# A two-layer decoder: stack loads ahead of value loads, normed rows and slots placed a step or more later, and four heads' scores at a time in the last two groups of each attention stage

## The reference, cut to what matters

```
x = layernorm(x + self_attention_0(x))          # "a0", causal, 16 heads of 16
x = layernorm(x + cross_attention_0(x, ctx))    # "c0", 1024 keys
x = layernorm(x + soft_moe(x))                  # rms-normed rows and slots, 8 experts
x = layernorm(x + self_attention_1(x))          # "a1", causal
x = layernorm(x + cross_attention_1(x, ctx))    # "c1", 1024 keys
y = layernorm(x, g1, b1)
x = x + attention_2(y); x = layernorm(x + token_moe(layernorm(x, g2, b2)))   # "a2", causal
```

## Time and profile before

| | us |
|---|---|
| median of 3 runs (2868.8 to 2877.04) | 2875.1 |
| the profiled execution, its own time | 2872.66 |
| its span | 2870.9 |

### The profile page before, as it was taken

The page is one execution under the profiler, slowest core; times in us unless marked ns, Lnnn a source line. Parts: engine busy times, 40 slices in busy tenths (PEclk is TensorE's granted clock), DMA queues, the critical chain, the costliest instruction groups (busy, mean ns, idle before and its releaser), DMA issues. The chain is left out here.

```text
span 2870.9 us, 47221 instructions
## 1 busy us (share of the span) xinstructions
PE 2526.0 (88%) x15793; PEld 1449.9 (51%) x15794; DVE 1494.8 (52%) x4176; ACT 1330.3 (46%) x2833; POOL 444.9 (15%) x687
## 2 busy tenths in 40 slices
PE   6999999999869889997899999999987994499991
PEld 3555544444334456675456544444444553266661
DVE  2555877888544500023555788777745654222224
ACT  2655466667744412111455567666664551022220
POOL 4222221101100000000123212202122001400004
PEclk8999999999999999999899999999998995599996
DMA  7544534233000022114644533242132317311103
GB/s 222 160 134 137 141 85 103 52 78 78 1 1 0 1 95 93 62 48 141 178 131 127 144 93 93 60 107 85 47 94 83 97 51 249 128 33 33 33 29 94
DMA packets 153825, 259.89 MB, mean 91 GB/s; under 512 B 22713, under 2 KB 96705, under 8 KB 149441
## 3 DMA queue, kind: packets, MB, share of 16 engines
q1 hardware_dynamic: 150544, 248.81, 29.9%
q0 software_dynamic: 3072, 8.39, 0.9%
HBM read 180.71 MB, written 81.53 MB: 91 GB/s over the span
## 5 line engine op out<-in xcount | busy, mean ns | idle before, releaser
L1444 ACT ACTIVATE second_p<-psum 128x512 f32<-128x512 f32 (+3 forms) x1024 | 461.5, 522 | 250.4 <-PE psum L1286 246.9
L1444 ACT ACTIVATE first_p<-psum 128x512 f32<-128x512 f32 (+3 forms) x768 | 366.7, 548 | 180.0 <-PE psum L1286 177.2
L1536 DVE TENSOR_REDUCE second_max_parts<-psum 128x1 f32<-128x512 f32 x512 | 323.0, 684 | 72.5 <-PE psum L1263 70.7
L1536 DVE TENSOR_REDUCE first_max_parts<-psum 128x1 f32<-128x512 f32 x512 | 323.0, 684 | 62.6 <-PE psum L1263 61.2
L1532 DVE CUSTOM_DVE_ANT_0 second_masked<-psum,mask_qk 128x384 f32<-128x384 f32 (+3 forms) x512 | 229.3, 488 | 198.1 <-PE psum L1263 168.0
L1298 PE MATMUL psum<-second_p,second_v_aug 128*32 128x512 f32 (+3 forms) x2048 | 236.0, 533 | 8.7 <-ACT second_p L1444 8.3
L1263 PE MATMUL psum<-second_k,second_q 64*128 64x512 f32 (+3 forms) x1024 | 201.0, 390 | 40.1 <-DMA second_k<-a_k_parts 27.4
L1276 PE MATMUL psum<-second_q,second_k 64*128 64x512 f32 (+3 forms) x1024 | 224.1, 434 | 3.3 <-DVE second_max_parts L1536 1.0
L1286 PE MATMUL psum<-second_shift_T,choose 64*128 64x512 f32 (+3 forms) x1024 | 196.9, 380 | 0.0
L1298 PE MATMUL psum<-first_p,first_v_aug 128*32 128x512 f32 (+3 forms) x1536 | 185.6, 555 | 10.5 <-ACT first_p L1444 10.5
L1276 PEld LDWEIGHTS psum<-second_q,second_k 64*128 64x128 f32 x1024 | 97.4, 186 | 186.0 <-ACT second_p L1444 78.1
(11 more groups left out here) (337 smaller groups left out, 3759.2 us busy)
## 6 DMA issues: line engine op xcount, KB each, us to landing
first_k<-c_k_parts SPq DMA_DIRECT2D x64, 256.0 KB, 4.7
second_q<-a_q_parts SPq DMA_DIRECT2D x128, 128.0 KB, 2.9
second_k<-a_k_parts SPq DMA_DIRECT2D x128, 128.0 KB, 2.9
second_k<-c_k_parts SPq DMA_DIRECT2D x64, 256.0 KB, 4.8
first_q<-a_q_parts SPq DMA_DIRECT2D x64, 128.0 KB, 2.9
first_k<-a_k_parts SPq DMA_DIRECT2D x64, 128.0 KB, 2.9
c_k_parts<-first_held SPq DMA_DIRECT2D x16, 512.0 KB, 3.0
first_q<-c_q_parts SPq DMA_DIRECT2D x64, 128.0 KB, 4.4
```

The lines of the kernel that those rows point to most:

```text
L1444: evacuated(act.activation(probs[tile % 2][:, 2 * h + p, q0:SEQ], bank[:, q0:SEQ], ACT.Exp, scale=scale), event)
L1536: evacuated(v.reduce_max(max_parts[n % 2][:, h, p, qt, k0 // BANK:k0 // BANK + 1], bank[:, 0:width], axis=AX_X), event)
```

## The change

It edits only the list of events. No operation is added or taken away.

```diff
--- before.py
+++ after.py
@@ -790,6 +790,10 @@
         steps = layer.key_tiles
         for t in range(steps):
             plan.append(("scores", n, (t, 0)))
+            if n + 2 >= groups:
+                if t == steps - 1 and n + 1 < groups:
+                    plan.append(("shift", n + 1, 0))
+                plan.append(("scores", n, (t, 1)))
             share(units, 2 * t + 1, 2 * steps)
             if t:
                 plan.append(("values", n, t - 1))
@@ -800,13 +804,14 @@
                     plan.append(("turn", n - 1, 0))
                 if n + 1 < groups:
                     plan.append(("augment", n + 1, 0))
+                if NB <= n + 3 < groups:
+                    plan.append(("load", n + 3, 0))
                 if n + 3 < groups:
                     plan.append(("vload", n + 3, 0))
-                if NB <= n + 3 < groups:
-                    plan.append(("load", n + 3, 0))
-            if t == steps - 1 and n + 1 < groups:
-                plan.append(("shift", n + 1, 0))
-            plan.append(("scores", n, (t, 1)))
+            if n + 2 < groups:
+                if t == steps - 1:
+                    plan.append(("shift", n + 1, 0))
+                plan.append(("scores", n, (t, 1)))
             share(units, 2 * t + 2, 2 * steps)
             if n + 1 < groups and t < 3:
                 plan.extend([("chain", n + 1, 2 * t), ("chain", n + 1, 2 * t + 1)])
@@ -2388,7 +2393,7 @@
             else:
                 pieces[GROUPS * (slot + 1)] = output_pieces(c0, slot) + rms_pieces(slot)
         pieces[GROUPS * BATCH + GROUPS - 1] += [("slot_stats", 0, 0), ("slot_root", 0, 0)]
-        pieces[GROUPS * BATCH + GROUPS] = [REST] + slot_pieces()
+        pieces[GROUPS * BATCH + GROUPS] = [REST, REST] + slot_pieces()
         soft_ctx = ctx.enter_context(ExitStack())
         c.rows = soft_ctx.enter_context(nc.sbuf_tensor("soft_rows_kept", [P, NT, D], F32))
         c.xT = soft_ctx.enter_context(nc.sbuf_tensor("soft_xT_kept", [P, DK, T], F32))
@@ -2430,11 +2435,14 @@
             whole = front_pieces(a2, slot, "x")
             pieces[first + 1] = output_pieces(c1, slot - BATCH)
             if b < BATCH - 1:
-                pieces[first + 2] = [REST, REST] + scaled_rows(slot) + whole[:5]
-                pieces[first + 3] = whole[5:]
+                pieces[first + 2] = [REST] * 3 + scaled_rows(slot) + whole[:4]
+                pieces[first + 3] = whole[4:]
             else:
-                pieces[first + 3] = scaled_rows(slot) + whole[:5]
-                pieces[first + 4] = whole[5:]
+                apply = pieces[first + 1].pop()
+                pieces[first + 2] = [REST, apply, REST, REST]
+                pieces[first + 3] = [REST, REST] + scaled_rows(slot) + whole[:3]
+                pieces[first + 4] = whole[3:7]
+                pieces[first + 5] = whole[7:] + pieces[first + 5]
             first += NG
             pieces[first + (b < BATCH - 1)] = output_pieces(a2, slot)
         fills = [(rows_dram[at:min(at + T, TILES * P), :], x_rows[0:min(T, TILES * P - at), :], rows_filled)
```

## The result

The changed kernel takes 2830.14 us, the median of 4 runs (2821.3 to 2832.26), beside 2874.65 for the kernel before in runs of the same time; the ratio is 0.9842 [0.9816, 0.9868], so 1.6% faster. The forecast of 2828 is 2 us off. The profiled execution took 2821.3 us (span 2819.5) and is the fastest of the four, so the two profiled executions differ by 51.4 us where the medians differ by 44.5. The experiment "after_again" says what the other 7 are. Medians leave out one disturbed execution, of rows_apart, which took 3262.4 us at a granted clock of 0.734.

What follows compares the result with a forecast made beforehand. The prediction took TensorE's work plus its waits to be the bound, with only waits and half clock to gain. Its terms, 5.3 + 6.2 + 4.4 + 12.0 + 2.0 + 0 + 11.0 + 3.5 = 44.4, took 2872.66 to 2828 us, range 2820 to 2837.

Steps and rivals of the forecast that it cites:

- slots 8 to 10: Second stage: TensorE's waits for VectorE's row operations shrink as turns move a step away; 6.2 us gained, ends 2.8 and 8.
- slot 11: Second stage: the 10.11 us stack wait goes, a wait of about 4.4 for rows stays; 12.0 us gained, ends 9 and 14.
- group 37: Output projections stop waiting right behind their turns, with a half step now between them; 2.0 us gained, ends 1 and 2.
- first tail: Groups 30 and 31 of "first": steps of 2.90 us become 2.05 to 2.2; 11.0 us gained, ends 7 and 12.4.
- second tail: Groups 46 and 47 of "second": seven waits of up to 0.89 us shrink; 3.5 us gained, ends 2 and 4.6.
- Part A: Stack transfers issued ahead of values on SyncE: small stack waits gain 5.3 us, ends 3 and 8; the 10.11 goes too.
- the clock behind them: TensorE's half-speed work after the waits at slots 8 to 10: 4.4 of 5.8 us gained, ends 0 and 5.8.
- Rival 2: Moved rows trade waits: evacuation costs 2 us per slot, clock still falls; terms 6.2 and 4.4 become 2.8 and 0; chance 0.15.
- Part C: The slots' first turn, 4.54 us behind VectorE's eight row operations: nothing gained, 0 us, ends -1 and 1.
- Part B: Last two groups of each stage, four heads' scores ahead of the values: 11.0 us in "first", 3.5 in "second".
- Rival 1: ScalarE becomes the bound in the last groups, steps stay near 2.5 us, 5 of 14.5 us gained; 2838, chance 0.12.
- Rivals 3 and 4: Stacks late by bandwidth, 10.11 stays, 2846, chance 0.04; early stack transfers collide with stores and contexts, slower, chance 0.03.

Runs made afterwards that it cites:

- after_again: The changed kernel unaltered, run again for a second profiled execution; 2827.09 us, ratio 0.9836.
- rows_apart: The changed kernel with the row operations of slots 8 to 11 and the group-20 slot further ahead of their turns; 2817.1 us, ratio 0.9810.
- a_only: The kernel before with only the stack transfers issued ahead of the value transfer; 2855.44 us, ratio 0.9929.
- a_d11: The kernel before with the stack transfers ahead of the value transfer and the slot-11 move, nothing else; 2854.28 us, ratio 0.9928.
- no_a: The changed kernel with values again loaded ahead of the stacks, all else kept; 2836.63 us, ratio 0.9875.
- d8_only: The kernel before with only the rows of slots 8 to 10 a step later and their turns two steps later; 2865.73 us, ratio 0.9972.
- outs_apart: The changed kernel with a step between turn and projection of every output piece in both stages; 2804.68 us, ratio 0.9776.
- b_only: The kernel before with only four heads' scores ahead of the values in the last two groups of each stage; 2858.84 us, ratio 0.9947.

## Why the prediction was right

The sum was 44.4 us; the medians of the two comparisons give 44.5 and 46.0, known to 7 and 5 us, so that an agreement to 0.1 is luck. Measured from shift turn to shift turn around each edit, in the two profiled executions, the terms came to 8.6 and 8.6 us (small stack waits, forecast 5.3), 8.4 and 9.8 (slots 8 to 10 with their clock, 10.6), 13.7 and 13.9 (slot 11 and group 37, 14.0), 9.1 and 9.4 (first tail, 11.0) and 3.8 and 3.8 (second tail, 3.5): 43.6 and 45.5 in all. The mechanisms held; one term was too small and two were too large, and they cancelled. Term by term:

**Part A, 5.3 for the small stack waits.** The waits of 1.17, 2.29 and 1.35 are gone. Left out of the change, part A costs 8.3 to 9.8 us, just above the high end of 8. The sum missed a sixth wait, 0.34 at 1572.48, and about 1 us around these four: their stretches are 1.4, 2.6, 1.6 and 0.6 us shorter in every kernel with part A, 6.2 for 5.2 of waits. The fifth, behind context transfers, is the larger miss. I gave it 0.5 us because one issue is moved past, and nothing for the clock of 0.68 behind it. In the changed kernel it is 0.39 and 0.38, the window behind it is at 1.00, and its stretch is 2.4 us shorter. In a_only and a_d11, with the same queue, it is 1.31 and 1.67 and its stretch isn't shorter at all. Why it is shorter in the whole change isn't settled.

**Slots 8 to 10, 6.2, and the clock behind them, 4.4.** The working of the first waits was exact, 4.42 - 2.94 = 1.48 and measured 1.48; the evacuation was 0.7 estimated and 0.89 measured, slot 10 went from 2.77 to 0 and 1.33 where I had 1.0. That makes 5.5 us instead of 6.2. Of the clock, the three stretches at half speed became one in the first execution (1.4 lost of 5.8, so 4.4 gained) and none in the second. Together the stretch became 8.4 and 9.8 us shorter, 6.8 in d8_only; forecast 10.6. Waits and clock would make 9.9 and 11.3, so some 1.5 us of them didn't arrive, and where they went isn't settled. Rival 2, with its evacuations of 2 us, is out. Its other half, half clock behind waits of 1.5, did occur. Five executions were profiled with these waits (two of the changed kernel, no_a, d8_only, outs_apart). Behind the waits of 1.48 and 0.89 the clock fell at four of ten places: slot 9 of the first execution, both slots of no_a (0.71 and 0.65), and slot 8 of d8_only, where three matmuls took 2.90 us. Behind slot 10, with its single wait of 1.33, it fell at none of five. The rule of the Trainium skill, "TensorE: Matmul & The Clock Gate", section "A second HAM failure mode: psum-queue depth-cycling", by which the clock swings where TensorE idles briefly and often between groups of matmuls, would have made the clock term 0. The windows at 1.00 behind slots 8 and 10 speak against that size, and the 0.72 behind slot 9 shows that such a fall does happen. The term of three parts in four was about right, without a reason that would have given it.

**Slot 11, 12.0, and group 37, 2.0.** 4.45 us of wait stayed (I had 4.4), with 4.49 us of work in the window at 0.54 (I took 2.4 us lost, it is about 2.1), and the projections' waits of 1.29 and 0.69 have no counterpart. 13.7 and 13.9 us shorter, forecast 14.0. What I didn't say: the change cures the 10.11 us twice. I put the gain down to part A while I also described how slot 7's norm leaves GpSimd's way, and had no sentence on the two being the same microseconds. For the total it made no difference; for someone who leaves out part A it does, since that costs 8 to 10 us and not the 18 that part A gains alone.

**Part C, 0.** The 4.54 is still there, as forecast.

**Part B, 11.0 and 3.5.** A step takes 2.12 us, in the middle of 2.05 to 2.2. Fourteen steps shorter by 0.78 are 10.9. Up to the last values of the stage the gain is 10.7, in both executions and in b_only. From group 30 to the start of "second" it is 9.1 and 9.4, though, and 8.6 in b_only, because the lower clock right behind (0.81 in the window from 784 us) gives some back: the first output projection there takes 3.38 us instead of 1.97. Groups 46 and 47 take 19.7 us instead of 23.5 from the shift turn to the last values, 3.8 for my 3.5. In all b_only gained 14.6 beside 14.5. Rival 1, a step of 2.5, is out. The drain copy in the way showed as the 0.20 and 0.41 above. ScalarE came closer to being the bound than the prediction's 1.96 us a step suggests: seven exponentials in 3.70 us, less one of 0.60, make some 2.07 for four in a step of 2.12.

Rivals 3 and 4 are out: no stack wait is new, and the waits of 1.17, 2.29, 1.35 and 10.11 went in a_only with the order of the queue alone.

**Two slips in the numbers.** The low ends add up to 23.8 us and not 24.8, which makes 2849 instead of 2848. And by the chances as listed, faster is 0.95 and within 0.3% 0.02, where the prediction has 0.94 and 0.03.

## What to carry to other kernels

Where a wait is the length of another engine's block of work, it is the distance between the block and its reader that counts, and what is left of it can be worked out from two rows (here to a hundredth of a microsecond at slots 8 and 9). But the block's work doesn't vanish: in rows_apart, with the reader covered, part of it came back at whatever else that engine serves. Before adding up the parts of a change, ask for each wait which parts would each remove it alone, and count it once. And a row whose idle time says "issue" is worth a look at the engines around it: nineteen of them, each about a microsecond, hid a gain as large as that of the largest part of this change (17 to 22 us beside 18.0 for part A alone).

## What the hardware showed that was not expected

The same two waits, 1.48 and 0.89 us, with the same four matmuls behind them, left the clock at full speed at slot 8 (window at 1.00) and brought it to half at slot 9 (0.72, the matmuls 3.35 us instead of 1.96) in one execution, and left it at full speed at both in the next. So the clock behind these waits differed from one execution to the next, with nothing in the profiles that would have told which it would be. Two profiled executions of one kernel differed by 7.8 us of span; the medians of two sets of four, 2830.1 and 2827.1, by 3.0.
